# One 400-column and one 200-column matmul per chunk become three of 200 columns into one accumulator

## What is computed

```python
hidden = x
for i in range(3):
    z = jnp.einsum('bmd,bnd->bmnd', x, hidden).reshape(B, -1, D)
    cur = jnp.einsum('bcd,co->bod', z, Ws[i]) + bs[i][None, :, None]
    cur = jax.nn.relu(cur)                      # 200 outputs
    if i != 2:
        hidden, direct = cur[:, :100, :], cur[:, 100:, :]
    else:
        direct = cur
    finals.append(direct)
return jnp.sum(jnp.concatenate(finals, axis=1), axis=-1)
```

## Time and profile before

| what | value |
|---|---|
| median of 3 runs | 2921.2 us (2920.04 to 2921.68) |
| the profiled execution's own time | 2919.57 us |
| its span | 2917.8 us |
| PE, PEld busy | 97%, 91% |
| DVE, ACT busy | 91%, 64% |
| granted TensorE clock, mean | 0.99 |

### The profile page before, as it was taken

How to read it: one execution, slowest core, us unless ns; L and a number is a source line. 1 busy time by engine, 2 the same in 40 slices (tenths; PEclk the granted TensorE clock), 3 DMA queues, 4 the chain that set the end, 5 groups by cost and what they waited for, 6 DMA issues and landing times.

```text
span 2917.8 us, 58694 instructions
## 1 busy us (share of the span) xinstructions
PE 2820.6 (97%) x18688; PEld 2666.4 (91%) x18688; DVE 2668.5 (91%) x2706; ACT 1873.7 (64%) x3850; POOL 1.1 (0%) x11
## 2 busy tenths in 40 slices
PE   1699999999999999999999999999999999999998
PEld 1699999999999999999999999999999999999998
DVE  3799999999999999999999999999999999999997
ACT  2466666666666666666666666666666666666665
POOL 0000000000000000000000000000000000000000
PEclk8899999999999999999999999999999999999999
DMA  8344444344444344344344344344444434444441
GB/s 193 84 130 107 107 128 110 106 127 113 104 125 117 104 124 118 104 120 121 104 118 124 104 117 125 104 112 129 104 109 128 108 107 127 111 106 126 113 106 53
DMA packets 256151, 333.83 MB, mean 114 GB/s; under 512 B 61346, under 2 KB 190990, under 8 KB 256014
## 3 DMA queue, kind: packets, MB, share of 16 engines
q1 hardware_dynamic: 256138, 333.67, 43.9%
HBM read 332.73 MB, written 8.37 MB: 117 GB/s over the span
## 4 chain that ended last, share of the span: by engine, by line
PE 95%; DMA 2%; DVE 1%; SPq 1%; ACT 1%; issue 0%; DVEq 0%; ACTq 0%
PE acc L589 62%; PE acc L590 28%; PE summed L608 4%; PE turned L601 1%; DMA xb<-x_by_unit 0%; DMA xb<-in_L_rec_b_dram 0%; DVE z_low L346 0%; DMA w_rows_again<-in_L_rec_W_dram 0%; DMA xb<-in_L_rec_W_dram 0%; DVE z L342 0%; DVE w_split L319 0%; DMA out_dram<-o_row 0%; ACT w_split L487 0%; ACT z_high L454 0%; SPq L194 0%
## 5 line engine op out<-in xcount | busy, mean ns | idle before, releaser
L589 PE MATMUL acc<-w_split,z_high 128*128 128x400 f32 (+1 forms) x8832 | 2672.9, 368 | 77.5 <-DVE z_low L346 71.6
L590 PE MATMUL acc<-w_split,z_low 128*128 128x200 f32 (+1 forms) x8832 | 2255.7, 255 | 0.0
L589 PEld LDWEIGHTS acc<-w_split,z_high 128*128 128x128 f32 (+1 forms) x8832 | 1661.5, 188 | 166.9 <-issue 159.3
L454 ACT ACTIVATE z_high<-z 128x1024 fp32r<-128x1024 f32 (+2 forms) x1152 | 1179.3, 1024 | 814.9 <-PE acc L590 737.5
L590 PEld LDWEIGHTS acc<-w_split,z_low 128*128 128x128 f32 (+1 forms) x8832 | 1690.9, 191 | 0.0
L346 DVE TENSOR_TENSOR z_low<-z,z_high 128x1024 fp32r<-128x1024 f32 (+2 forms) x1152 | 1353.4, 1175 | 129.3 <-ACT z_high L454 129.2
L342 DVE TENSOR_TENSOR z<-hid,xb 128x1024 f32<-128x1024 f32 (+1 forms) x1024 | 1213.8, 1185 | 59.7 <-DMA xb<-x_by_unit 50.9
L475 ACT ACTIVATE hid<-turned 96x512 f32<-96x512 f32 x256 | 149.1, 582 | 132.2 <-PE turned L601 132.2
L478 ACT ACTIVATE hid<-turned 32x128 f32<-32x128 f32 x768 | 204.6, 266 | 8.9
L608 PE MATMUL summed<-s,group_b 128*4 128x100 f32 (+1 forms) x768 | 150.1, 277 | 1.4 <-ACT s L470 1.4
L351 DVE TENSOR_TENSOR s<-acc,half 128x200 f32<-128x200 f32 x384 | 137.8, 359 | 10.5 <-ACT half L459 10.5
(11 more groups left out here) (20 smaller groups left out, 13.5 us busy)
## 6 DMA issues: line engine op xcount, KB each, us to landing
xb<-x_by_unit SPq DMA_DIRECT2D x384, 384.0 KB, 4.8
x_right<-x_by_unit SPq DMA_DIRECT2D x384, 136.5 KB
xb<-x_by_unit SPq DMA_DIRECT2D x384, 128.0 KB, 5.7
xb<-x_by_unit SPq DMA_DIRECT2D x128, 336.0 KB
xb<-x_by_unit SPq DMA_DIRECT2D x128, 84.0 KB
x_left<-x_by_unit SPq DMA_DIRECT2D x384, 19.5 KB
out_dram<-o_row SPq DMA_DIRECT2D x256, 1.6 KB
xb<-in_L_rec_W_dram SPq DMA_DIRECT2D x6, 600.0 KB, 9.2
```

Source lines behind the costliest of these rows:

```text
L454: nc.scalar.activation(z_high[slot][0:rows, 0:n * T], z[slot][0:rows, 0:n * T], ACT.Copy).then_inc(high, 1)
L589: nc.tensor.matmul(a[:, 0:2 * O], z_high[slot][0:rows, tok], w, start=(c == 0), stop=False, skip_group_check=True)
L590: last = nc.tensor.matmul(a[:, 0:O], z_low[slot][0:rows, tok], w[:, 0:O], start=False, stop=(c == chunks - 1), skip_group_check=True)
```

## The change

Each chunk now has three matmuls of 200 columns, all into columns 0 to 199 of `acc`: `z_high` by the rounded weights, `z_low` by the rounded weights, `z_high` by the rest. The accumulator then holds the whole sum. `half`, `second_half`, `sums`, `dup` and `relu` go, and ACT reads `acc` itself in `outputs`, which stands where `second_half` stood. `acc_free` waits for ACT's two semaphores in place of `s_in`.

```diff
             def acc_free(l, u):
-                pe.wait_ge(s_in[l], u)
+
+                if l < 2:
+                    pe.wait_ge(factors_in[l], u)
+                pe.wait_ge(direct_in[l], u)
...
-                    nc.tensor.matmul(a[:, 0:2 * O], z_high[slot][0:rows, tok], w, start=(c == 0), stop=False, skip_group_check=True)
-                    last = nc.tensor.matmul(a[:, 0:O], z_low[slot][0:rows, tok], w[:, 0:O], start=False, stop=(c == chunks - 1),
+                    nc.tensor.matmul(a[:, 0:O], z_high[slot][0:rows, tok], w[:, 0:O], start=(c == 0), stop=False, skip_group_check=True)
+                    nc.tensor.matmul(a[:, 0:O], z_low[slot][0:rows, tok], w[:, 0:O], start=False, stop=False, skip_group_check=True)
+                    last = nc.tensor.matmul(a[:, 0:O], z_high[slot][0:rows, tok], w[:, O:2 * O], start=False, stop=(c == chunks - 1),
                                             skip_group_check=True)
                 last.then_inc(freed, 1)
...
-            def sums(l, u):
-                dve.wait_ge(half_in[l], u + 1)
-                nc.vector.tensor_tensor(s[l][:, :, 0:HID], acc[l][:, 0:O].rearrange("p (h o) -> p h o", o=HID), half[l][:, :, :], ALU.add)\
-                  .then_inc(s_in[l], 1)
...
-            def second_half(l, u, last):
+            def outputs(l, u, last):
 
                 act.wait_ge(freed, RING + last + 1)
-                nc.scalar.activation(half[l][:, :, :], acc[l][:, O:2 * O].rearrange("p (h o) -> p h o", o=HID), ACT.Copy)\
-                  .then_inc(half_in[l], 1)
...
+                if l < 2:
+                    nc.scalar.activation(s[l][:, 0, 0:HID], acc[l][:, 0:HID], ACT.Copy)
+                    nc.scalar.activation(s[l][:, 0, HID:HID + TAIL_ROWS - TAIL].rearrange("p (j q) -> p j q", q=TAIL),
+                                         acc[l][:, MAIN:HID].unsqueeze(1).to_broadcast([P, TAIL_M - 1, TAIL]), ACT.Copy)\
+                      .then_inc(factors_in[l], 1)
+                    nc.scalar.activation(s[l][:, 1, 0:HID], acc[l][:, HID:O], ACT.Relu).then_inc(direct_in[l], 1)
+                else:
+                    nc.scalar.activation(s[l][:, :, :].rearrange("p h o -> p (h o)"), acc[l][:, 0:O], ACT.Relu).then_inc(direct_in[l], 1)
```

More of the change, by code:

```diff
@@ L93, in cin_kernel @@
         s = {0: sb("s0", [P, 2, P]), 1: sb("s1", [P, 2, P]), 2: sb("s2", [P, 2, HID])}
-        half = {l: sb(f"half{l}", [P, 2, HID]) for l in range(3)}
         ident = sb("ident", [P, P])
@@ L123, in cin_kernel @@
         freed = sem("freed")
[L124 to L127, removed]
+        factors_in = [sem(f"factors_in{l}") for l in range(2)]
+        direct_in = [sem(f"direct_in{l}") for l in range(3)]
         turned_in = [sem(f"turned_in{l}") for l in range(2)]
@@ L377, in _ @@
                     lows(1, 1, L0_ROWS, L0_CHUNKS)
-                    sums(0, 0)
-                if k == 3:
-                    sums(0, 1)
             dve.wait_ge(w_low_done, 1 + 2 * GROUPS)
@@ L392, in _, with period @@
             lows(at + 4, slot_of(at + 4), L0_ROWS, L0_CHUNKS)
-            sums(1, 0)
-            sums(0, 2)
-            def period(n, par, base, sl, layer0=True, sum2=True, last_low=True):
+            def period(n, par, base, sl, layer0=True, last_low=True):
                 def slot(p):
@@ L409, in period @@
                 lows(base + 2, slot(2), P, group_chunks(2))
-                if sum2:
-                    sums(2, n - 2)
                 q = 4
@@ L425, in period @@
                 lows(base + q + 1, slot(q + 1), P, group_chunks(1))
-                sums(1, n)
                 product12(2, n - 1, 1 - par, 3, base + q + 3, slot(q + 3))
                 lows(base + q + 2, slot(q + 2), P, group_chunks(2))
-                if layer0:
-                    sums(0, n + 2)
-            period(1, 1, first(1), first(1) % RING, sum2=False, last_low=False)
+            period(1, 1, first(1), first(1) % RING, last_low=False)
             with dve.Fori(0, (UNITS - 4) // 2) as i:
@@ L440, in _ @@
             product12(2, UNITS - 1, 1, 0, at, slot_of(at))
-            sums(2, UNITS - 2)
             for g in range(1, GROUPS):
@@ L445, in _ @@
             lows(at + 3, slot_of(at + 3), P, group_chunks(3))
-            sums(2, UNITS - 1)
         @block.scalar
@@ L497, in _ @@
                     highs(1, 1, L0_ROWS, L0_CHUNKS)
[L498 to L501, removed]
+                    outputs(0, 0, 0)
                 if k == 3:
@@ L504, in _ @@
                     results(0, 0)
[L505 to L508, removed]
+                    outputs(0, 1, 1)
                 if k == 7:
@@ L516, in _ @@
             highs(at + GROUPS, slot_of(at + GROUPS), L0_ROWS, L0_CHUNKS)
[L517 to L520, removed]
+            outputs(1, 0, at + 3)
+            outputs(0, 2, at + 4)
             def period(n, par, base, sl, layer0=True, before0=True, before2=True):
@@ L534, in period @@
                 if before2:
-                    second_half(2, n - 2, base - 1)
+                    outputs(2, n - 2, base - 1)
                 results(1, n - 1)
@@ L543, in period @@
                     q = 5
-                if before2:
-                    relu(2, n - 2)
                 if before0:
@@ L549, in period @@
                 highs(base + q + 1, slot(q + 1), P, group_chunks(1))
-                second_half(1, n, base + 3)
+                outputs(1, n, base + 3)
                 highs(base + q + 2, slot(q + 2), P, group_chunks(2))
                 if layer0:
-                    second_half(0, n + 2, base + 4)
+                    outputs(0, n + 2, base + 4)
                 if before2:
@@ L556, in period @@
                 highs(base + q + 3, slot(q + 3), P, group_chunks(3))
-                dup(1, n)
-                relu(1, n)
             period(1, 1, first(1), first(1) % RING, before2=False)
@@ L567, in _ @@
             hidden(1, UNITS - 1, 1)
-            second_half(2, UNITS - 2, at - 1)
+            outputs(2, UNITS - 2, at - 1)
             for g in range(GROUPS):
@@ L571, in _ @@
             results(1, UNITS - 1)
-            relu(2, UNITS - 2)
             results(2, UNITS - 2)
-            second_half(2, UNITS - 1, at + 3)
-            relu(2, UNITS - 1)
+            outputs(2, UNITS - 1, at + 3)
             results(2, UNITS - 1)
@@ L594, in acc_free @@
             def acc_free(l, u):
-                pe.wait_ge(s_in[l], u)
+                if l < 2:
+                    pe.wait_ge(factors_in[l], u)
+                pe.wait_ge(direct_in[l], u)
             def transpose(l, u):
-                pe.wait_ge(tail_dup[l], u + 1)
+                pe.wait_ge(factors_in[l], u + 1)
                 if not (isinstance(u, int) and u == 0):
@@ L603, in sum_over_d @@
             def sum_over_d(l, u):
-                pe.wait_ge(relu_done[l], u + 1)
+                pe.wait_ge(direct_in[l], u + 1)
                 if not (isinstance(u, int) and u == 0):
```

3 lines of the change are left out of this document (removed).

## The result

The changed kernel takes 3285.2 us in the median of four runs (3284.4 to 3289.5) against 2921.4 us for the kernel before: a ratio of 1.125 (95% interval 1.123 to 1.127), or +364 us. The forecast was 3185 us with a range of 3110 to 3300, and slower with a chance of 0.91.

The account below looks back on a forecast made before the run. The prediction took PE's stream of 8832 chunks as the bound: 2919.57 us, +265 for a third load-bound matmul per chunk, +0.6 at start-up, -0.7 at the end, gave 3185 us, range 3110 to 3300.

Parts of the forecast that it names:

- What bounds the kernel: Whole kernel: PE bounds it, busy 97% of the span with 95% of the chain; DVE and ACT wait for PE.
- The 2531 us of work foretold for DVE: DVE: 384 sums go, 137.8 us, leaving 2531 us of work off the path; no gain by itself.
- How the cycle of a chunk works: TensorE, each chunk: 400 columns hide the next load and decide; under 200 columns the load, 0.108 us, decides.
- 3 x 0.108 us: Chunk's three 200-column matmuls: the load decides three times, 0.324 us against 0.294, +265 us over 8832 chunks.
- The lower end of my range: Chunk's loads: lowest reading in which the load decides, 0.107 us each, 0.321 us a chunk, +238 us.
- The forecast's band of 0.107 to 0.112 us: Loads in the matmul stream: 0.107 to 0.112 us each, covering 3158 to 3290 us, chance 0.74.
- Waits and ACT: ACT's reads and semaphore waits: 232 us of reads in place of 292, hidden behind PE; nothing late.
- The faster rival: Matmul stream: columns decide, 0.093 us a 200-column matmul, 0.279 us a chunk, -130 us, 2790 us; chance 0.08.
- The 2602 us: Matmul stream by the skill's isolated-matmul rule: 86 ns per 200 columns, three 258 ns, a chunk cheaper by 36 ns.
- The fixed price per matmul: Matmul stream: each change of weights costs 0.022 us, so the third matmul adds 194 us, 3114 us; chance 0.07.
- Loads that wait for a turn: Matmul stream: each load waits a little for a matmul's turn, 0.118 us a load, 3450 us; chance 0.10.

Follow-up runs that it names:

- the evacuation alone: Kernel before, its 400- and 200-column matmuls kept, with ACT reading the accumulator itself and DVE's sums gone: 2916.7 us, ratio 0.9988 to before.
- widths 240 and 300: Changed kernel with its three matmuls of 240 or 300 columns in place of 200: 3306.6 and 4005.3 us, one run each.
- same operand twice: Changed kernel with second and third matmul exchanged, so two matmuls of z_high stand in a row: 3284.5 us, ratio 1.125 to before.
- third apart: Three matmuls of 200 columns, the third into columns 200 to 399, with the evacuation of before: 3286.6 us, ratio 1.126 to before.
- grouped: Kernel before with all 400-column matmuls of a group first, then all its 200-column ones: 2923.6 us, ratio 1.0009.
- Cutting the short matmul in two: Kernel before with its 200-column matmul of z_low split into two of 100 columns, each with its own load: 7128.7 us, one run at 1.2 GHz.

## Why the prediction was right, and where its size was off

- *What bounds the kernel*: right. PE held 95% of the chain and holds 97% now; DVE's sums went and the evacuation alone is worth 4 us. The 2531 us of work foretold for DVE came out as 2618.7: the rows of the sums are 137.8 us, but DVE's rows overlap (in the kernel before, its four largest groups, 1353.4, 1213.8, 138.4 and 137.8 us, add up to more than its 2668.5 us), so its busy time fell by 50 us only. Its share, 80%, came out as foretold because the span was longer as well, which is luck. It cost nothing, since DVE was off the path. PE's share is 97%, not the near 99% foretold.
- *How the cycle of a chunk works*: right in the main, and shown from several sides. The longer of load and columns decides (widths 240 and 300), the load is the floor, it is paid for each matmul whatever operand is in the array (same operand twice), and neither the columns written (third apart) nor the switch of operands (grouped) costs anything. One part needs a word more: a load starts right behind the matmul's start only where the columns decide; where the loads decide, it follows the load before it.
- *3 x 0.108 us*: this term was mis-sized. It measured 3 x 0.1117. That is 0.011 us a chunk, or 98 us, of the 100 between 3185 and 3285. I took 0.108 as "the distance already seen where a load is followed by the next load with 200 columns streaming". But before, each such load had an idle load path ahead of it, since the one before it had ended long before under the 400 columns. The starts of the loads in the changed kernel show it: over the 405 uninterrupted bursts between 189 us and 2.7 ms of the span, the median of the first distance is 0.108, of the second 0.110 and at every later place 0.112. In the kernel before, every second distance is 0.108 (108.3 to 108.5 ns in the mean at each place of a burst). The grouped kernel shows the same, with 0.108 for the first load after those of the 400 columns and 0.112 from the third on. Why a load after a rest is cheaper stays open. The lower end of my range was at one load alone; I set no bound by loads that follow each other without rest. The forecast's band of 0.107 to 0.112 us took the result in at its upper end, but no row stood behind that 0.112, so this was in part luck.
- At 1.2 GHz a load takes 0.2133 us, twice 0.1067, with nothing on top. The Trainium skill's page "TensorE: Matmul & The Clock Gate", section "Wait — 56ns, not 53.3ns?", gives the distance between the starts of matmuls of 128 columns: 53.3 + 2.5 ns at 2.4 GHz and 106.7 at 1.2. It speaks of matmuls there and not of loads. Twice that is 111.6 and 213.3 ns, my estimate by the page, and the distances of the loads in the traces, 111.7 and 213.3 ns, agree with both. That a load of fp32r is two passes of 128 columns is a reading that fits; no run here looked inside one.
- *Waits and ACT*: right. ACT's two reads of 100 columns took 237 and 257 ns, that of 24 columns 183 and that of 200 columns 338, where I had taken 270, 270, 205 and 325, and all of it is hidden.
- *The faster rival* (0.093 us a matmul by its columns) fell: the starts that spoke for it were the matmuls' turns. Cutting the short matmul in two shows that plainly, since its halves start 0.08 us apart while their loads start 0.34 apart. The 2602 us that the prediction worked out from the Trainium skill's rule for isolated matmuls fell too: 200 columns, each matmul behind a load of fp32r, took 0.112 us and not 0.086. *The fixed price per matmul* fell with the widths, since 240 columns cost no more than 200. *Loads that wait for a turn* (0.118) is refuted by 0.1117, and by the steady pace of the loads beside that of the matmul starts.

## What to carry to other kernels

A matmul is worth its columns only while they are longer than the load of the next stationary operand; in a stream of loads and matmuls, cost each step as the larger of the two, and count what lies bare. In this kernel that was 0.112 us for 128 columns of fp32r, so matmuls of fewer than about 240 columns pay the difference (240 and 300 columns took 0.112 and 0.138 us, some 0.013 above one column per cycle), and an accumulation that saves a copy elsewhere has to be weighed against it. Take the price of a load from loads that directly follow each other; one that comes after a rest looks cheaper.

## What the runs showed of the hardware that was not expected

- The clock. Three matmuls of 200 columns every 0.335 us ran at 2.4 GHz. The same with 176 or 128 columns, and 400 + 100 + 100 columns with three loads, ran at 1.2 GHz throughout, and doubled the time: 6091, 6076 and 7129 us. Each of the three ran once. In these kernels TensorE was busy by the page for 98 or 99% of the span, and for 90% or more in every one of its 40 slices but the first, so the busy share gave no warning. Narrowing the matmuls of the changed kernel from 200 columns to 176 raised the time from 3285 to 6091 us. What it is that keeps the clock down was not tried further.
- The record of the clock can be missing where it matters: in these runs the page has no line for it and gives a mean of 1.000. The durations of an untouched instruction tell it: a transpose takes 276 ns in the changed kernel and 415, 435 and 456 ns in these three.
- A bf16 load of 128 columns hides under 200 columns at 0.086 us a matmul; an fp32r load doesn't (0.112).
